# Projections of later pairs with both parts of x side by side, and a norm moved behind the last keys' split

## What is computed

```python
# x (8, 112, 512), ctx (8, 375, 512), w* (512, 512), gate (8, 512), experts (8, 2048, 512) and (8, 512, 1024)
def attention(x, k_cache, v_cache, wq, wk, wv, wo):
    q = jnp.einsum('bsd,ed->bse', x, wq)
    k = jnp.concatenate([k_cache, jnp.einsum('bsd,ed->bse', x, wk)], axis=1)
    v = jnp.concatenate([v_cache, jnp.einsum('bsd,ed->bse', x, wv)], axis=1)
    attn = jax.nn.softmax(jnp.einsum('bqd,bkd->bqk', q, k) / math.sqrt(512), axis=-1)
    return jnp.einsum('bqd,ed->bqe', jnp.einsum('bqk,bkd->bqd', attn, v), wo)

x = x + attention(_layernorm(x), ctx, ctx, wq, wk, wv, wo)
x = x + experts_of_top_2(_layernorm(x))     # weights of the two by softmax of x @ gate.T
```

## Time and profile before

| | |
|---|---|
| median of 3 runs | 456.49 us (456.36 to 456.56) |
| the profiled execution | 456.27 us, of which its span in the trace is 454.5 us |
| granted TensorE clock | 0.994 of full speed |
| PE busy | 441.0 us (97%) |
| DVE, ACT, POOL busy | 343.8, 253.5, 98.7 us |
| pair bodies in the trace | from about 20 us to 161 us; experts from about 170 us on |

### The profile page before, as it was taken

How to read it: one execution, slowest core, us unless ns; L and a number is a source line. 1 busy time by engine, 2 the same in 40 slices (tenths; PEclk the granted TensorE clock), 3 DMA queues, 4 the chain that set the end, 5 groups by cost and what they waited for, 6 DMA issues and landing times.

```text
span 454.5 us, 7156 instructions
## 1 busy us (share of the span) xinstructions
PE 441.0 (97%) x2530; PEld 373.3 (82%) x2530; DVE 343.8 (76%) x644; ACT 253.5 (56%) x414; POOL 98.7 (22%) x128
## 2 busy tenths in 40 slices
PE   8999999999999999999999999999999999999991
PEld 6979888878888678888888888888888888888880
DVE  5867546556645678898988988988988888888850
ACT  4566434514623666666566566666666656656621
POOL 6060071334427253003003003003003003003002
PEclk9999999999999999999999999999999999999997
DMA  8996984434545465976766856856956846856203
GB/s 274 349 259 186 278 216 139 142 51 140 195 115 226 129 224 153 341 236 194 249 199 176 272 185 199 263 165 205 276 156 204 276 157 198 284 164 196 56 0 51
DMA packets 26911, 88.39 MB, mean 194 GB/s; under 512 B 2560, under 2 KB 8704, under 8 KB 26880
## 3 DMA queue, kind: packets, MB, share of 16 engines
q1 hardware_dynamic: 23296, 80.13, 54.4%
q0 software_dynamic: 3584, 7.88, 8.7%
HBM read 73.55 MB, written 14.45 MB: 194 GB/s over the span
## 4 chain that ended last, share of the span: by engine, by line
PE 85%; DVE 4%; DMA 3%; ACT 2%; issue 2%; POOL 1%; SPq 1%; POOLq 0%; ACTq 0%; DVEq 0%
PE T L412 13%; PE PJ L412 13%; PE PJ L413 6%; PE T L413 6%; PE SC L509 3%; PE SC L510 3%; PE SC L511 3%; PE T L245 3%; PE PJ L232 2%; PE PJ L234 2%; PE PJ L233 2%; PE SC L262 2%; PE SC L266 2%; PE SC L264 2%; DMA wTs<-in_weights 2%
## 5 line engine op out<-in xcount | busy, mean ns | idle before, releaser
L897 DVE TENSOR_TENSOR ul<-ng,uh 128x1536 fp32r<-128x1536 f32 x64 | 112.5, 1757 | 3.1 <-ACT uh L647 1.9
L647 ACT ACTIVATE uh<-ng 128x1536 fp32r<-128x1536 f32 x64 | 94.8, 1481 | 0.3 <-DMA ng<-in_units 0.3
L412 PE MATMUL T<-eb,uh 128*128 128x512 f32 x248 | 88.7, 397 | 0.0
L412 PE MATMUL PJ<-eb,uh 128*128 128x512 f32 x248 | 88.7, 397 | 0.0
L1366 POOL DMA_INDIRECT out<-ys,yidx x16 | 27.8, 1738 | 194.3 <-ACT ys L821 191.8
L413 PE MATMUL PJ<-eb,ul 128*128 128x256 f32 x248 | 69.7, 281 | 0.0
L413 PE MATMUL T<-eb,ul 128*128 128x256 f32 x248 | 69.6, 281 | 0.0
L412 PEld LDWEIGHTS PJ<-eb,uh 128*128 128x128 f32 x248 | 46.6, 188 | 11.2
L412 PEld LDWEIGHTS T<-eb,uh 128*128 128x128 f32 x248 | 46.6, 188 | 11.2
L413 PEld LDWEIGHTS T<-eb,ul 128*128 128x128 f32 x248 | 46.8, 189 | 1.3
L413 PEld LDWEIGHTS PJ<-eb,ul 128*128 128x128 f32 x248 | 46.7, 188 | 1.3
(11 more groups left out here) (240 smaller groups left out, 918.5 us busy)
## 6 DMA issues: line engine op xcount, KB each, us to landing
ng<-in_units SPq DMA_DIRECT2D x64, 768.0 KB, 4.5
vs<-in_ctxn SPq DMA_DIRECT2D x8, 768.0 KB, 5.2
kTs<-in_ctxT SPq DMA_DIRECT2D x8, 750.0 KB, 5.0
slots<-zero SPq DMA_DIRECT2D x8, 514.0 KB, 12.9
xe<-slots SPq DMA_DIRECT2D x8, 514.0 KB, 4.3
wTs<-in_weights SPq DMA_DIRECT2D x8, 512.0 KB, 8.0
out<-x_all SPq DMA_DIRECT2D x8, 224.0 KB, 3.9
x_all<-in_x SPq DMA_DIRECT2D x1, 896.0 KB, 19.0
```

The source lines that it names most:

```text
L412: nc.tensor.matmul(o[:, :].rearrange("p (h s) -> p h s", h=2), wh, both[:, k, :, :], start=k == 0, stop=False)
L647: nc.scalar.activation(o, i, ACT.Copy).then_inc(s, 1)
L897: v.tensor_tensor(o, whole, hi.bitcast(F32), ALU.subtract).then_inc(s, 1)
```

## The change

Both parts of x for a pair now lie side by side in one tile `xb`, `[128, 4, 2, 224]`; `xTh` and `xTl` are views of it. In the bodies of pairs 0, 1 and 2 the chunks 0, 1 and 2 are computed by a new `pe_proj_wide`: for each of the chunk's two row blocks and each k, one matmul of `wTh` by both parts (448 columns) and one of `wTl` by the high part (224 columns), the first row block in bank SC[0], the second in SC[1]. The columns 224 to 447 of a bank then hold high weights by low x and must be added to the columns 0 to 223. ACT copies them out (`half_pj`, two copies to `pt`), DVE adds them (`sum_pj`, two sums to `qf`), and `hi_pj` and `lo_pj` read `qf` in place of the bank. The next chunk takes both banks again, so chunks 1, 2 and 3 wait for the sums of the chunk before (`pj_sum`). Chunk 3, and all four before pair 0, stay as they were.

The first norm of a pair, `x2_norms(A, 0)`, leaves its place ahead of `lo_pj` of chunk 2 and goes into the next body, behind `lo_pj` of chunk 3.

```diff
+        pt = sb("pt", [128, 2, 2 * S], F32)
+        qf = sb("qf", [128, 2, 2 * S], F32)
...
-        xTh = sb("xTh", [128, KT, 2 * S], F32R)
-        xTl = sb("xTl", [128, KT, 2 * S], F32R)
+        xb = sb("xb", [128, KT, 2, 2 * S], F32R)
+        xTh, xTl = xb[:, :, 0, :], xb[:, :, 1, :]
...
+        def pe_proj_wide(c):
+            w = c // 2
+            for h in range(2):
+                bank = SC[h]
+                m = 2 * (c % 2) + h
+                ms = slice(128 * m, 128 * m + 128)
+                for k in range(KT):
+                    nc.tensor.matmul(bank[:, 0:4 * S].rearrange("p (u t) -> p u t", u=2), wTh[w][:, k, ms], xb[:, k, :, :],
+                                     start=k == 0, stop=False)
+                    last = nc.tensor.matmul(bank[:, 0:2 * S], wTl[w][:, k, ms], xTh[:, k, :], start=False, stop=k == KT - 1)
+            last.then_inc(pj, 1)
...
                 pe.wait_ge(x_lo, A + 4)
-                pe_proj(0, SC[0])
+                pe_proj_wide(0)
...
-                pe.wait_ge(expd, B + 1)
-                pe_proj(1, SC[1])
+                pe.wait_ge(pj_sum, 6 * p + 2)
+                pe_proj_wide(1)
...
-                pe.wait_ge(pj_lo, 4 * p + 5)
-                pe_proj(2, SC[0])
+                pe.wait_ge(pj_sum, 6 * p + 4)
+                pe_proj_wide(2)
...
-                pe.wait_ge(pj_lo, 4 * p + 6)
+                pe.wait_ge(pj_sum, 6 * p + 6)
                 pe_proj(3, SC[1])
...
+            def half_pj(p, c):
+                act.wait_ge(pj, 4 * p + c + 1)
+                for h in range(2):
+                    copy(pt[:, h, :], SC[h][:, 2 * S:4 * S], pj_copy)
...
             def hi_pj(p, c, bank):
-                act.wait_ge(pj, 4 * p + c + 1)
-                v = bank[:, 0:4 * S].rearrange("p (m t) -> p m t", m=2)
+                if p and c < 3:
+                    act.wait_ge(pj_sum, 2 * (3 * p - 3 + c) + 2)
+                    v = qf[:, :, :]
...
+                    half_pj(p + 1, 0)
                     hi_c(A + 2, 0)
                     hi_pj(p + 1, 0, SC[0])
...
                     hi_o(A, 0, T[1])
+                    half_pj(p + 1, 1)
                     hi_c(A + 3, 1)
                     hi_pj(p + 1, 1, SC[1])
                 hi_o(B, 1, T[2])
                 if more:
+                    half_pj(p + 1, 2)
                     hi_v(A + 2, 0)
...
+            def sum_pj(p, c):
+                n = 2 * (3 * p - 3 + c)
+                dve.wait_ge(pj_lo, 4 * p + c)
+                for h in range(2):
+                    dve.wait_ge(pj_copy, n + h + 1)
+                    v.tensor_tensor(qf[:, h, :], SC[h][:, 0:2 * S], pt[:, h, :], ALU.add).then_inc(pj_sum, 1)
...
                 lo_pj(p, 3, SC[1])
                 if p:
+                    x2_norms(A - 2, 0)
                     x2_norms(A - 1, 1)
...
                 if more:
+                    sum_pj(p + 1, 0)
                     lo_c(A + 2, 0)
                     lo_pj(p + 1, 0, SC[0])
...
                 if more:
+                    sum_pj(p + 1, 1)
                     lo_c(A + 3, 1)
...
                 x2_stats(A, 0, PJ[0])
                 if more:
-                    x2_norms(A, 0)
+                    sum_pj(p + 1, 2)
                     lo_pj(p + 1, 2, SC[0])
                 x2_stats(B, 1, PJ[1])
```

More of the change, by code:

```diff
@@ L206, in build_kernel @@
         pj, pj_hi, pj_lo = sem("pj"), sem("pj_hi"), sem("pj_lo")
+        pj_copy, pj_sum = sem("pj_copy"), sem("pj_sum")
         c_hi, c_lo = sem("c_hi"), sem("c_lo")
@@ L664, in hi_x @@
                 copy(xTh[:, :, a * S:a * S + S], bank[:, 0:KT * S].rearrange("p (k t) -> p k t", k=KT), x_hi)
+            def half_pj(p, c):
+                act.wait_ge(pj, 4 * p + c + 1)
+                for h in range(2):
+                    copy(pt[:, h, :], SC[h][:, 2 * S:4 * S], pj_copy)
             def hi_pj(p, c, bank):
-                act.wait_ge(pj, 4 * p + c + 1)
-                v = bank[:, 0:4 * S].rearrange("p (m t) -> p m t", m=2)
+                if p and c < 3:
+                    act.wait_ge(pj_sum, 2 * (3 * p - 3 + c) + 2)
+                    v = qf[:, :, :]
+                else:
+                    act.wait_ge(pj, 4 * p + c + 1)
+                    v = bank[:, 0:4 * S].rearrange("p (m t) -> p m t", m=2)
                 m = 2 * (c % 2)
@@ L937, in lo_x @@
                    xTh[:, :, a * S:a * S + S], x_lo)
+            def sum_pj(p, c):
[4 more added lines that the diff above has]
+                    v.tensor_tensor(qf[:, h, :], SC[h][:, 0:2 * S], pt[:, h, :], ALU.add).then_inc(pj_sum, 1)
             def lo_pj(p, c, bank):
                 dve.wait_ge(pj_hi, 4 * p + c + 1)
-                w = bank[:, 0:4 * S].rearrange("p (m t) -> p m t", m=2)
+                w = qf[:, :, :] if p and c < 3 else bank[:, 0:4 * S].rearrange("p (m t) -> p m t", m=2)
                 m = 2 * (c % 2)
```

## The result

The changed kernel takes 454.83 us (median of 22 runs, 454.25 to 456.87); the kernel before took 456.26 on the same chip (22 runs, 455.21 to 457.71). The ratio is 0.9972 with a 95% interval of 0.9963 to 0.9981: 1.28 us or 0.28% faster by the ratio (0.87 to 1.69 us by its interval), 1.43 by the medians. The forecast was 1.05 us, 455.4. The profiled execution took 454.57 us (before 456.27), its span is 452.7 (454.5).

A forecast was written before the change was run, and what follows sets the result against it. PE, busy 441.0 of 454.5 us, was taken as the bound. Savings of 1.35 + 0.75 less 0.5 and 0.55 made 1.05 us, so 455.4 us was forecast, range 454.3 to 456.9.

The forecast's parts named there:

- Wide chunks: Nine chunks in the bodies of pairs 0 to 2: 2.52 us each for 2.67, 1.35 us saved on PE's path.
- a floor under the narrow products: 224-column products on PE pay a minimum: 0.111 us each, where 512 columns cost 0.23, 2.1 times as much, not 2.3.
- Halves: Added ACT copies and DVE sums delay pair 0's output projection, costing 0.5 us; pairs 1 and 2 lose nothing.
- the margin of 0.5 us: Slack in pair 1 between A's `oTl` being done (82.4) and PE wanting it (83.0) for the output projection.
- The norm: Moved behind the last keys' low part, it lets pair 2's scores follow their transposes after 0.32 us: gain 0.75.
- the hole: PE's 1.07 us between transposes at 97.35 and scores at 98.42, waiting for the last keys' low part on DVE.
- The give-back: Later scatter landings delay the second norm to 98.4 and x in pair 2, returning 0.55 of 1.15 us gained.
- the 5.48: Time in us from `rows` done to the first scatter transfer's start, taken as unchanged when `rows` comes 1.7 later.
- rival A: The scatter isn't moved by `rows`, so x is never late and the 0.55 us stays: 454.9 us; chance 0.22.

The follow-up runs named there:

- the run with the norm 1.42 us later: Changed kernel with pair 1's second load of context values issued only after A's product with wo; 455.84 against 456.52 us for the kernel before, ratio 0.9978.

## Why the prediction was right, and where it was not

- **Wide chunks, 1.35 us.** Right, if small: pairs stand at 0.313 to 0.315, chunks take 2.52 to 2.59, 0.15 to 0.18 is saved in each and some 1.5 in nine. The reason given, a floor under the narrow products, is argued and not shown. A fixed cost of every product, whatever its width, explains the same rows, and no run tells the two apart. An estimate: the line through 224 columns at 0.111 and 512 at 0.23 has 0.018 us of such a cost, so that eight products fewer in a chunk save 0.15 too. It puts 448 columns at 0.204 and the experts' pair at 0.354; scaling by width, with the floor for the narrow one only, puts them at 0.20 and 0.345; measured were 0.205 in blocks and 0.351. A floor there is, for eight products of 8 columns take 0.10 each (pair 0 after, 41.65 to 42.47), but 224 columns lie above it. The estimate from the figures of the Trainium skill ("TensorE: Matmul & The Clock Gate", "Back-to-back issue gap") was 0.296 a pair. The page calls that formula the gap of a single isolated matmul, and for a stream of loads and matmuls it gives about 131 ns at 512 columns. The trace, with 0.23 us for 512, agrees with neither; the rows were the better guide.
- **Halves.** Copies are listed at 0.35 and sums at 0.38, forecast 0.36 and 0.38. Pair 0 paid 0.57, forecast 0.5, and the run with early weights took it away. Pairs 1 and 2 paid nothing, and the margin of 0.5 us was right too: a chain 1 us longer cost 0.48 and 0.51.
- **The norm, 0.75 us.** Right: 0.76 in the trace of the change, 0.79 of way with the norm alone. What the prediction did not say is that this part carries the other. With the hole in place, the gains of pairs 0 and 1 vanish in it.
- **The give-back, 0.55 us: wrong.** The step that failed is "With `rows` 1.7 later and the same 5.48, the landings are 96.6 and 98.3". `rows` was later as worked out (1.88 us), but the 5.48 were not a distance: some 3.3 us belong to it, the rest was the wait for a load. The first transfer started at 85.92, 0.13 later, and the fourth 0.81 later; the landing let the second norm start at 97.50, and x was in time. The price was sound, only its condition did not arise: in the run with the norm 1.42 us later it cost 1.07, so some 0.35 are free, and a norm at 98.4 would have cost about 0.55 by that estimate.
- **The sum.** 1.5 for the chunks, 0.76 for the hole, less 0.57: 1.69, and the way shows 1.67. The forecast's 1.35 + 0.75 - 0.5 - 0.55 was 1.05; the missing 0.6 is nearly all the give-back. The times show 1.28 by the ratio, between the two, and their interval of 0.87 to 1.69 holds both: that nothing was given back rests on the traces.
- **The number.** 454.83 is within the range and under the 455.6 that stood for faster, but not within the forecast's own band, 455.1 to 455.8. It is the number of rival A, 454.9, to which 0.22 was given. A's result came, and A's reason in part: the 5.48 us did not all start from `rows`, yet the run with the rows first shows that the transfer does follow them. That the late rows met the load at its end and so cost next to nothing was luck.

## What to carry to other kernels

An engine's gain ahead of a wait that hangs on a transfer is not a gain until that wait is moved off its path: look for the next such wait before pricing any edit, and make both edits together. A stretch that the chain calls "issue" is no constant; look at what the DMA queues, that of instructions too, do in it before it is added to a moved start. And new work put on a helper engine costs where something long stands behind it in the queue: here the roundings and low parts of `wo`'s weights, which could as well go ahead.

## What was not expected of the hardware

- A packet of 0.01 MB of the queue "instruction" ahead of an indirect transfer: with one the scatter starts 3.6 us behind the cast of its rows, without one 0.97 to 1.15, and a 768 KB load queued ahead of the packet made it 5.8.
- A 768 KB load beside row transfers of 112 rows made their landing 8.2 us for 6.6 in one kernel, 10.9 for 7.0 in another.
- Alternating matmuls of 448 and 224 columns take 0.21 and 0.105 us, in blocks 0.205 and 0.11: the sum is the same to 0.01 us.
